# Relative rows of two images from block-diagonal tables, projections three units ahead, and evenly spaced score groups in a four-block attention kernel

## The reference, cut to what matters

```
attn  = einsum('bqd,bkd->bqk', q * scale, k)
rel_h = einsum('bhwc,hkc->bhwk', r_q, Rh)      # Rh[y, k] = rel_pos_h[y - k + 31]
rel_w = einsum('bhwc,wkc->bhwk', r_q, Rw)
attn  = attn + rel_h[:, :, :, :, None] + rel_w[:, :, :, None, :]
out   = softmax(attn) @ v ;  out @ w_proj + b_proj
```

## Time and profile before

| | us |
|---|---|
| median of 3 runs | 7617.72 (7615.88 to 7628.22) |
| the profiled execution, its own time | 7618.39 |
| its span from first to last instruction | 7616.5 |
| PE busy | 6794.8 (89%) |
| DVE busy | 5195.2 (68%) |
| ACT busy | 3773.4 (50%) |
| POOL busy | 1973.8 (26%) |

### The profile page before, as it was taken

The page is one execution under the profiler, slowest core; times in us unless marked ns, Lnnn a source line. Parts: engine busy times, 40 slices in busy tenths (PEclk is TensorE's granted clock), DMA queues, the critical chain, the costliest instruction groups (busy, mean ns, idle before and its releaser), DMA issues. The chain is left out here.

```text
span 7616.5 us, 152912 instructions
## 1 busy us (share of the span) xinstructions
PE 6794.8 (89%) x54592; PEld 4022.6 (53%) x54592; DVE 5195.2 (68%) x7583; ACT 3773.4 (50%) x6953; POOL 1973.8 (26%) x2311
## 2 busy tenths in 40 slices
PE   3999999999977999389999999996776899999999
PEld 2555555555545555255555555552332555555555
DVE  3666666666655788366666666664887777777776
ACT  0444444444522677134444444442111777777777
POOL 3334434434221000244344344331110000000000
PEclk7899999999988999589999989998676999999999
DMA  6776776676548998587767767753222555555553
GB/s 159 163 144 136 137 147 135 135 145 140 97 150 218 171 146 127 136 175 137 152 130 142 149 128 142 151 102 99 70 87 83 126 137 138 124 136 133 125 143 92
DMA packets 500291, 1025.76 MB, mean 135 GB/s; under 512 B 80103, under 2 KB 276392, under 8 KB 460280
## 3 DMA queue, kind: packets, MB, share of 16 engines
q1 hardware_dynamic: 452406, 932.06, 56.4%
q0 software_dynamic: 47360, 86.53, 7.1%
HBM read 670.93 MB, written 358.93 MB: 135 GB/s over the span
## 5 line engine op out<-in xcount | busy, mean ns | idle before, releaser
L1484 DVE TENSOR_REDUCE a_nmp<-a_S 128x2 f32<-128x1024 f32 x1536 | 1877.3, 1224 | 973.7 <-PE a_S L1341 961.3
L1621 ACT ACTIVATE a_PROB<-a_T 128x512 f32<-128x512 f32 x3072 | 1667.8, 595 | 1658.3 <-PE a_T L1320 1635.2
L1213 POOL CAST a_RF<-a_RL 32x512 fp32r<-32x512 f32 x1536 | 1302.3, 848 | 374.1 <-DVE a_RL L1537 284.9
L2366 DVE CUSTOM_DVE_ANT_0 a_X<-a_S,a_mask 128x1024 f32<-128x1024 f32 x768 | 921.4, 1219 | 416.3 <-PE a_S L2276 410.8
L1354 PE MATMUL a_O<-a_PROB,a_V 128*32 128x512 f32 x6144 | 956.4, 699 | 0.5 <-ACT a_PROB L1621 0.5
L2426 ACT ACTIVATE a_PROB<-a_T 128x512 f32<-128x512 f32 x1536 | 834.5, 600 | 208.3 <-PE a_T L2290 203.0
L1316 PEld LDWEIGHTS a_T<-a_QW,a_KW 64*128 64x128 f32 x3072 | 306.5, 193 | 1148.7 <-issue 1142.8
L1316 PE MATMUL a_T<-a_QW,a_KW 64*128 64x512 f32 x3072 | 808.9, 521 | 69.4 <-ACT a_PROB L1621 69.2
L2290 PE MATMUL a_T<-a_ident,a_X 128*128 128x128 f32 x6144 | 832.9, 279 | 4.0
L2290 PEld LDWEIGHTS a_T<-a_ident,a_X 128*128 128x128 f32 x6144 | 666.9, 141 | 274.4 <-issue 262.1
L1341 PEld LDWEIGHTS a_S<-a_KV,a_QV 64*128 64x128 f32 x6144 | 637.8, 199 | 134.4
(11 more groups left out here) (167 smaller groups left out, 8504.9 us busy)
## 6 DMA issues: line engine op xcount, KB each, us to landing
a_QV<-a_part_rows SPq DMA_DIRECT2D x384, 256.0 KB, 7.4
a_rel_rows<-a_RF SPq DMA_DIRECT2D x96, 1024.0 KB, 9.1
a_K<-part_rows SPq DMA_DIRECT2D x576, 128.0 KB, 4.0
a_part_rows<-a_part SPq DMA_DIRECT2D x48, 1024.0 KB, 16.0
a_QV<-a_part_rows SPq DMA_DIRECT2D x384, 128.0 KB, 7.9
a_QV<-a_rel_rows SPq DMA_DIRECT2D x384, 128.0 KB, 6.5
a_QW<-a_rel_rows SPq DMA_DIRECT2D x192, 256.0 KB, 8.5
a_mask<-L_mask SPq DMA_DIRECT2D x48, 1024.0 KB, 7.3
```

Source lines behind the costliest of these rows:

```text
L1213: nc.gpsimd.tensor_copy(dst, src).then_inc(permuted, 1)
L1484: nc.vector.tensor_reduce(nmp[:, qh, c, 2 * pr:2 * pr + 2, kh], S[:, pr], AX.X, ALU.max).then_inc(s_done, 1)
L1621: nc.scalar.activation(PROB[:, s % PRING, 2 * pr + sd], T[:, slot(("st", s, pr, sd))], ACT.Exp).then_inc(t_act, 1)
L2366: nc.vector.tensor_tensor_reduce(out=X[:, v % 2, c, g], in0=S[:, sd].rearrange("p a b -> p (a b)"), in1=mask[:, n % 2, g, c], scale=1.0, s ...
```

## The change

In `attend_rel` the relative rows of two images are made together in even units: eight `rel` jobs of eight products each, four with row tables and four with column tables. The tables become block-diagonal over the four heads (64 rows of values, 64 rows of zeros beside the keys), so that one product has 128 contraction rows, 128 output rows and 64 moving columns (32 queries of each of two images). Odd units have no `rel` job. The copies out of the ring write their rows in final order, so `permute`, `RF`, `QC` and its moves are gone; the table store becomes 16 transfers of 256 KB for a pair of images, eight per way, with DRAM scratch for four images. q, k and v are made three units ahead rather than two, v in one job. The ring order is now one list over all units without empty places. The programs of SyncE and GpSimd, which had loops, are written out.

In `attend_rot` the score groups move to other places among TensorE's steps, the output projection from step 4 to 5, VectorE takes the two operations of a group in the other order, and its four operations on the output (`turn`, `invert`, `divide`, `turn_back`) stand between groups.

```diff
-    JOBS = {0: ("qk0",), 1: ("qk1",), 2: ("v0",), 3: ("v1",), 4: ("nm10",), 5: ("nm11",), 6: ("wo10",), 7: ("wo11",),
-            8: ("rel0",), 9: ("rel1",), 10: ("rel2",), 11: ("rel3",), 12: ("nm00",), 13: ("pad", "nm01"), 14: ("wo00",),
-            15: ("wo01",)}
+    EVEN = {0: ("qk0",), 1: ("qk1",), 2: ("rel0",), 3: ("rel1",), 4: ("rel2",), 5: ("nm10",), 6: ("nm11",), 7: ("rel3",),
+            8: ("wo10",), 9: ("wo11",), 10: ("v",), 11: ("rel4",), 12: ("nm00", "rel5"), 13: ("nm01", "rel6"),
+            14: ("wo00", "rel7"), 15: ("wo01",)}
+    ODD = {0: ("qk0",), 1: ("qk1",), 3: ("v",), 4: ("nm10",), 5: ("nm11",), 6: ("wo10",), 7: ("wo11",), 12: ("nm00",),
+           13: ("nm01",), 14: ("wo00",), 15: ("wo01",)}
...
+    def slot(e):
+        return AT[e] % RING
...
+        def table_lines(r, i):
+            way, p = divmod(r, 4)
+            if way == 0:
+                return RL[:, :, i, 256 * p:256 * p + 256].rearrange("p e (y x) -> p y e x", x=SIDE)
+            return RL[:, :, i].rearrange("p e (y x) -> p x e y", x=SIDE)[:, 8 * p:8 * p + 8]
...
+            def store_tables(v, way):
+                sp.wait_ge(t_dve, made(f"rel{4 * way + 3}", v, "dve"))
                 alone(sp)
+                for e in range(2):
+                    for g in range(G):
+                        sp.dma_start(rel_rows[(v + e) % 4, way, g], plain(RL[g:P:G, e])).then_inc(rel_stored, 16)
...
+            def section(u):
+                v, first = u + 2, u % 2 == 0 and u + 2 < UNITS
+                if u + 3 < UNITS:
+                    store_parts(u + 3)
+                if first:
+                    store_tables(v, 0)
+                if v < UNITS:
+                    sp.wait_ge(t_ready, upto(u, ("st", CHUNKS - 1, 1, 1), "pe"))
...
+                    query_rows(v, 0)
+                if u + 4 < UNITS:
+                    load_behind(u + 4)
+                if first:
+                    store_tables(v, 1)
+                if v < UNITS:
+                    sp.wait_ge(rel_stored, 2 * TABLES * (v // 2 + 1))
+                    alone(sp)
+                    table_rows(v, 0)
+                    sp.wait_ge(t_ready, upto(u, ("st", STEPS - 1, 1, 1), "pe"))
+                    alone(sp)
+                    keys(v)
+                    query_rows(v, 1)
+                    table_rows(v, 1)
...
             def relative(v, r, to):
-                pe.wait_ge(qc_moved, 64 * (v + 1))
+                pe.wait_ge(t_dve, made("qk1", v + 1, "dve"))
                 alone(pe)
+                way, p = divmod(r, 4)
                 for a in range(8):
-                    for half in range(2):
-                        x = 8 * r + a
-                        at = 64 * half
-                        last = nc.tensor.matmul(T[at + 32:at + 64, to, 64 * a:64 * a + 64], tab_d[:, x],
-                                                QC[:, :, half * BANK + x:(half + 1) * BANK:SIDE], start=True, stop=True)
...
+                    x = 8 * p + a
+                    if way == 0:
+                        table, queries = tab_h[:, G * (SIDE - 1 - x):G * (2 * SIDE - 1 - x)], whole[:, :, SIDE * x:SIDE * x + SIDE]
+                    else:
+                        table, queries = tab_d[:, x].rearrange("p c g -> p (c g)"), whole[:, :, x:TOKENS:SIDE]
+                    last = nc.tensor.matmul(T[:, to, 2 * SIDE * a:2 * SIDE * a + 2 * SIDE], table, queries,
+                                            start=True, stop=True)
...
             # ScalarE, before rel0 and rel4 of a pair
+                    if r % 4 == 0:
+                        need(act, rel_stored, TABLES * (2 * before + r // 4), solo=True)
+                    ins = nc.scalar.copy(table_lines(r, 0), table_bank(to))
...
             # attend_rot, TensorE
+                if not isinstance(u, int) or u:
+                    outputs(u - 1, 1 - par, CHUNKS - 1)
+                for kc in range(CHUNKS):
+                    transposed(u, par, kc, 0)
+                    if kc == 6:
+                        ahead(3)
+                    transposed(u, par, kc, 1)
                     if kc:
                         outputs(u, par, kc - 1, mine)
+                    if kc in (0, 2, 4):
+                        ahead(kc // 2)
```

More of the change, by code:

```diff
@@ L916, in attend_rel @@
[L916 to L923, removed]
-    def kind(n):
-        return "dve" if n in BY_DVE + BY_BOTH else "act"
@@ new lines, in attend_rel, with exists @@
+    ODD = {0: ("qk0",), 1: ("qk1",), 3: ("v",), 4: ("nm10",), 5: ("nm11",), 6: ("wo10",), 7: ("wo11",), 12: ("nm00",),
+           13: ("nm01",), 14: ("wo00",), 15: ("wo01",)}
+    RELS = tuple(f"rel{r}" for r in range(8))
+    BY_DVE = ("qk0", "qk1", "v", "nm00", "nm01", "nm10", "nm11")
+    def exists(n, u):
+        if n in ("qk0", "qk1", "v"):
+            return u + 3 < UNITS
+        if n in RELS:
+            return u + 2 < UNITS
+        if n in ("nm00", "nm01"):
+            return u + 1 < UNITS
+        return u > 0 or n not in ("wo10", "wo11")
@@ L944, in upto @@
+    SEQ += [(UNITS, "wo10"), (UNITS, "wo11")]
+    AT = {n: i for i, n in enumerate(SEQ)}
+    def kind(n):
+        return "dve" if n in BY_DVE + RELS else "act"
+    TALLY, _seen = {}, {"pe": 0, "act": 0, "dve": 0}
+    for _e in SEQ:
+        for k in _seen:
+            _seen[k] += k == "pe" or k == kind(_e[1]) or (k == "act" and _e[1] in RELS)
+        TALLY[_e] = dict(_seen)
     def upto(u, n, k):
-        mine = used(u)
-        return base(u, k) + tally(mine[:mine.index(n) + 1], k)
+        return TALLY[(u, n)][k]
@@ new lines, in _ @@
+            load(0)
+            load_behind(1)
+            store_parts(0)
+            load_behind(2)
+            store_parts(1)
+            store_tables(0, 0)
+            sp.wait_ge(part_stored, 16)
+            alone(sp)
+            query_rows(0, 0)
+            keys(0)
+            query_rows(0, 1)
+            store_tables(0, 1)
+            sp.wait_ge(rel_stored, 2 * TABLES)
+            alone(sp)
+            table_rows(0, 0)
+            table_rows(0, 1)
+            load_behind(3)
@@ new lines, in _ @@
+            store_parts(2)
+            sp.wait_ge(part_stored, 32)
+            alone(sp)
+            sp.wait_ge(k_moved, KEY_ROWS)
+            alone(sp)
+            for half in range(2):
+                sp.wait_ge(rows_moved[half], ROWS)
+                alone(sp)
+            query_rows(1, 0)
+            table_rows(1, 0)
+            keys(1)
+            query_rows(1, 1)
+            table_rows(1, 1)
+            for b in range(IMAGES):
+                sp.dma_start(stream[b], x_in[b]).then_inc(copied, 16)
@@ L1229, in unit @@
-            def unit(hg, b, par, before, more, follows):
-                u = hg * IMAGES + b
-                if follows:
-                    place(u + 1, 1 - par)
-                if more:
+                nc.gpsimd.tensor_copy(V[:, v % 2, :, :, 0:DIM], VS[:, v % 2]).then_inc(v_placed, 1)
+            pool.wait_ge(ones_placed, 32)
+            for v in range(3):
+                for half in range(2):
+                    separate(v, half)
+                if v == 0:
+                    place(0)
@@ L1235, in unit @@
+            for u in range(UNITS):
+                if u + 1 < UNITS:
+                    place(u + 1)
+                if u + 3 < UNITS:
                     for half in range(2):
-                        separate(u + 2, half, upto(u, f"qk{half}", "dve"))
-                if before is not None:
+                        separate(u + 3, half)
+                if u == 0:
+                    pool.wait_ge(copied, 16 * IMAGES)
+                else:
                     for m in range(2):
-                        store(before, 1, m, upto(u, f"wo1{m}", "act"))
```

465 lines of the change are left out of this document (158 added, 307 removed).

## The result

The changed kernel takes 7304.36 us (median of 4 runs, 7301.99 to 7312.62) against 7616.80 for the kernel before beside it: a ratio of 0.959, 95% interval 0.957 to 0.961. The forecast was 7334 us. The spans of the profiled executions are 7300.2 and 7616.5, so 316 us went. From the start of the first row maximum (VectorE) to that of the last, the first relative stage fell from 1918.2 to 1796.2 us and the second from 1904.1 to 1783.9, together 242; in the rotary stage, from the first to the last masked maximum, 1678.5 became 1612.9, 66 less. Both parts of the change gave something.

The account below looks back on a forecast made before the run. Relative stages were taken to last as long as TensorE's program, slowed by a clock falling behind relative jobs. Sum: 7618.4 - 260 - 31 + 10 + 26 - 29 = 7334 us; range 7235 to 7530.

Parts of the forecast that it names:

- Relative pairs: Relative stages: a pair of units takes 152.05 us against 163.84, over eleven pairs in each of two stages: -260 us.
- last units: Units 21 to 23 of both relative stages: steps without a job get shorter, unit 21 loses `qk` and `v`: -31 us.
- Column jobs: `rel4` to `rel7`, reading every 32nd query: priced at 2.29 us each, bounds 1.94 and 2.6.
- Table rows after `rel7`: Odd units' straight scores wait for table rows, about 1.2 us late, 22 times: +26 us, bounds 0 and +110.
- Strided copies: Copies by `table_lines`: if strided writes doubled the 0.69 us remainder, TensorE would see it only through the table rows' wait.
- Opening: Start of both relative stages: added projections and relative jobs against two reordering runs gone: +10 us, between -58 and +36.
- Rotary: Rotary stage: score groups' waits go, last values' product gets a new wait of 0.62 us: -29 us over 95 units.
- A: Rival: the clock still falls behind each relative job, 7637 us, or 7712 with the double v falling too; chance 0.08.
- B: Rival: the clock falls only where jobs grew longer, both v jobs and three steps with two jobs: 7523 us; chance 0.15.
- C: Rival: table rows become the bound, transfers and the keys behind them landing some 10 us late: 7528 us; chance 0.13.
- D: Rival: no new waits, neither table rows nor the rotary stage's last values' product wait: 7249 us; chance 0.12.

Follow-up runs that it names:

- e8_corners: Changed kernel with rel0 to rel3 of steady units replaced by an old job's 24 products, with 16 or 128 contraction rows, in four strips or one: 7557.89 us (one run).
- e2_shapes: Changed kernel with steady units' rel0 and rel1 cut to 32 contraction rows, rel2 and rel3 to 32 output rows: 7254.94 us (one run).
- e1_old_rotary: Changed kernel with the rotary stage (`attend_rot`) of the kernel before, so only the relative stages are changed: 7362.16 us, ratio 0.9661.

## Why the prediction was right, and where its terms were off

The mechanism held: the clock fell because of the old products' shape, and v's was the right row to go by. Its sum was 284 us of gain, and the spans differ by 316. That the sum came so near is in part luck: the gain of the pairs and last units was put 42 us too high, and against it stand table rows at 26 us that did not come, a rotary gain 37 too low and an opening 12 too dear.

*Relative pairs, -260, and last units, -31.* From the output projection of unit 0 to that of unit 20 a pair took 163.8 and 162.3 us before in the two stages, and 153.4 and 152.2 after; the forecast was 152.05. From unit 0 to the last output projection both stages together lost 249 us, against 291. Inside this, four sizes were off. Column jobs were priced some 0.4 us too high (2.29 against 1.97 in the rows above and 1.86 to 1.89 in the three that follow, from the job's start to the next product's): 88 x 0.4 = 35 us to the good. Against it stand the waits of 34 us for the column copies, some 11 falls behind v, 19 us, and a second stage that had lost less to the clock before (1.5 us less a pair, some 17 us). With these the forecast is 256. The price of 2.29 came from products of 32 output rows, in which a strided read shows; in these, with the 128 output rows of v's, it does not.

*Table rows after `rel7`, +26.* This step failed: it kept the 12.7 us from a store to its table rows, measured on two transfers of 1024 KB (9.1 us from issue to landing), for eight of 256 KB (2.4 us), and took their number as an addition. In the queue the rows follow after 9.5 us in all, so nothing waits but unit 21. With the term the relative part was forecast at 265 against 249, so the one error hides part of the other.

*Strided copies.* The prediction said that a doubled remainder would be seen only through the table rows. It is seen sooner, by the transposed scores of the next step, which need the remainder's place in the ring. The Trainium skill's "SBUF — State Buffer" (Door 1: The DMA port swizzle) has it that each move to another 16-byte line costs. The copies agree (1.1 and 1.19 us against 0.59 and 0.69, and short again with runs of 32 bytes). TensorE's strided reads agree where 32 output rows are loaded: eight products of 128 x 32 take 1.92 us in `e8_corners` (the row at 904.57), which reads queries 128 bytes apart, and 1.08 in `e2_shapes`, which reads them one after the other, both at a clock of 1.00. With 128 output rows the stride does not show (2.04 against 2.00), perhaps because the weight load is the longer part; that was not separated.

*Opening, +10.* First to last, everything outside the stretches above comes to -2 us. TensorE waits 21 us for table rows at each opening, and still its first output projection in the first stage is only 0.9 us later (282.7 against 281.8).

*Rotary, -29.* The mechanism was right and the wait mis-sized. Score groups wait 8.5 us where they waited 88.2; the last values' product waits 0.34 us, not 0.62. From the start of the transposes to the values that need them it is 2.01 us, where the earlier trace rows gave 2.29:

```profile
6701.09 1.09 PE L2234 MATMUL a_T<-a_ident,a_X 128*128 128x128 f32 x8
6702.11 0.64 PE L2245 MATMUL a_O<-a_PROB,a_V 128*32 128x256 f32 x8
6703.10 0.64 PE L2245 MATMUL a_O<-a_PROB,a_V 128*32 128x256 f32 x8 [0.34 <-ACT a_PROB L2368]
```

The rows are of the kernel after, in TensorE's timeline. The stage gave 66 us in the profile and 58 in `e1_old_rotary`; over it TensorE's idle time fell from 106.8 to 43.0 us, which is 64 of the 66. The stage before, to be read beside the window above (length, busy TensorE):

```profile
5911.70:7590.20 1678.50, 1571.70 (x14052) 955.86 (x14052) 1300.22 (x2294) 1304.81 (x2378) 90.13 (x94) 0.99 0.53 130
```

*The rivals.* A did not come: values behind 128-row products stay at 1.06, but for one of 176. The Trainium skill's "TensorE: Matmul & The Clock Gate" (Why this matters for your kernels), which led there, counts idle gaps. The two falls behind the keys' waits agree; but here the clock also fell behind stretches without a gap, in 22 of 22 jobs of `e8_corners`, and packing small products into strips does not cure it (11 of 22). B came in a small part: behind v, 11 times of 42, nine of them in odd units, and behind none of the steps with two jobs. C did not come: the keys' two waits are 10.3 us in all. D was half right: neither of the two feared waits had its size, but the copies' waits took their place.

## What to carry to other kernels

Where TensorE is busy throughout and the clock is below 1.00, look at which products stand just ahead of the slow stretch and how many contraction rows they fill; rewriting them to use all 128, with zeros if need be, was worth 1.7 us a job here. When a copy is to write in final order, let TensorE scatter its columns in the bank, which was free here, and give the copy runs of 32 bytes. A step moved to make room should be checked for what it covered: one values' product and the empty places of a ring each carried tens of us.

## What the runs showed of the hardware that was not expected

Two streams of 24 products (48 instructions in one strip) alike in count, columns and output rows differ in 16 or 128 contraction rows, and in their step of the unit: behind the one the clock is at its lower level in 22 of 22 cases (values 1.93 us), behind the other in none of 22 (1.06). At one and the same step, v with 32 rows is followed by slow values 20 times of 20, with 96 rows nine times. A job of eight products with 64 moving columns takes 1.08 us for 128 contraction and 32 output rows, 1.99 for 32 and 128, and 2.00 for 128 and 128. A moving operand read every 32nd element cost TensorE nothing at 128 output rows (2.04 against 2.00 us) and 0.84 us at 32 (1.92 against 1.08). A bank written every eighth column, at 128 output rows, cost nothing (291 against 290 ns).
